# A pre-norm attention and mixture-of-experts layer: four groups of extra PE waits removed

## The reference

```
x = x + attention(layernorm(x))
x = x + ffn(layernorm(x))

attention: 16 heads of 64, q, k, v = split(xh @ Wqkv + bqkv)      # one 64 x 192 matrix for all heads
    att = (q @ k.T / 8) * tril(ones, k=-1)                         # a masked score is 0, not -inf
    out = softmax(att) @ v,  then @ Wr + br
ffn:  w = softmax(flat @ router_w + router_b), all but the top 2 of 8 set to 0
    gelu(flat @ sw1 + sb1) @ sw2 + sb2                             # shared expert, 1024 -> 2048 -> 1024
    + sum over e of w[:, e] * (gelu(flat @ rw1[e] + rb1[e]) @ rw2[e] + rb2[e])
```

## Time and profile before

| | us |
|---|---|
| median of 3 runs | 4011.67 |
| the three runs | 3928.25, 4011.67, 4037.73 |
| time of the profiled execution | 3928.25 |
| its span (slowest core, first to last instruction) | 3926.7 |
| spans of the 8 cores | 3921.7 to 3926.7 |

### The profile page before, as it was taken

The page is one execution under the profiler, slowest core; times in us unless marked ns, Lnnn a source line. Parts: engine busy times, 40 slices in busy tenths (PEclk is TensorE's granted clock), DMA queues, the critical chain, the costliest instruction groups (busy, mean ns, idle before and its releaser), DMA issues.

```text
span 3926.7 us, 45908 instructions; the slowest of 8 cores (3921.7 to 3926.7 us)
## 1 busy us (share of the span) xinstructions
PE 2935.5 (75%) x15380; PEld 1345.2 (34%) x15380; DVE 1167.6 (30%) x2358; ACT 855.8 (22%) x1354; POOL 28.9 (1%) x55
## 2 busy tenths in 40 slices
PE   2454454555455445665999999999999999999997
PEld 0122222222222222222444444444444444444443
DVE  5222222222222222253132333333233333333332
ACT  0232222332222223101212121121212112122210
POOL 0000000000000000000000000000000000000000
PEclk7555555555555555686999999999999999999998
DMA  2100000000000000050022220502222050221302
GB/s 87 33 1 1 1 1 1 1 1 1 1 1 1 1 1 1 1 86 1 1 48 39 44 44 1 87 1 44 43 38 49 1 86 1 44 43 33 54 1 86
DMA packets 7087, 98.81 MB, mean 25 GB/s; under 512 B 1860, under 2 KB 2260, under 8 KB 2260
## 3 DMA queue, kind: packets, MB, share of 16 engines
q0 software_dynamic: 3984, 77.81, 11.8%
q1 hardware_dynamic: 2884, 18.06, 1.3%
HBM read 165.10 MB, written 8.39 MB: 44 GB/s over the span
## 4 chain that ended last, share of the span: by engine, by line
PE 70%; DVE 12%; issue 8%; ACT 7%; DMA 1%; DVEq 1%; ACTq 0%; SPq 0%; POOL 0%
PE PM L746 26%; PE PM L835 25%; PE PS L438 6%; DVE SMASK L418 5%; ACT PT L423 4%; PE PS L399 4%; ACT PT L409 3%; DVE AVN L455 2%; PE PTR L462 2%; PE PS L342 2%; PE PS L505 2%; DVE RZ L450 1%; PE PS L368 1%; PE PS L359 1%; DVE XLN L248 1%
## 5 line engine op out<-in xcount | busy, mean ns | idle before, releaser
L746 PE MATMUL PM<-XLN,W 128*128 128x512 bf16 x4608 | 1020.7, 385 | 0.7 <-DVE WSB L704 0.7
L835 PE MATMUL PM<-H1G,W 128*128 128x512 bf16 x4608 | 999.0, 379 | 0.0
L763 ACT ACTIVATE H1G<-PM,B1C 128x512 bf16<-128x512 f32 x576 | 395.9, 687 | 1611.6 <-PE PM L746 1611.6
L746 PEld LDWEIGHTS PM<-XLN,W 128*128 128x128 bf16 x4608 | 455.3, 99 | 562.6 <-issue 33.6
L835 PEld LDWEIGHTS PM<-H1G,W 128*128 128x128 bf16 x4608 | 450.9, 98 | 543.7
L438 PE MATMUL PS<-VA,PT 128*128 128x65 bf16 x2560 | 176.2, 242 | 349.5 <-ACT PT L423 349.5
L812 DVE TENSOR_TENSOR H1G<-H1G,WB 128x512 bf16<-128x512 bf16 x512 | 217.8, 425 | 686.3 <-ACT H1G L763 686.3
L850 DVE TENSOR_TENSOR XRES<-XRES,PM 128x512 f32<-128x512 f32 x288 | 198.2, 688 | 652.1 <-PE PM L835 652.1
L399 PE MATMUL PS<-QT,KT 64*128 64x512 bf16 x640 | 322.4, 600 | 73.0 <-ACT PT L409 72.4
L409 ACT ACTIVATE PT<-PS 128x512 bf16<-128x512 f32 x384 | 209.0, 594 | 566.6 <-PE PS L399 566.1
L418 DVE TENSOR_TENSOR SMASK<-PS,MASKS 128x512 f32<-128x512 f32 x256 | 176.9, 691 | 457.9 <-PE PS L399 285.1
(11 more groups left out here) (99 smaller groups left out, 826.7 us busy)
## 6 DMA issues: line engine op xcount, KB each, us to landing
W<-w1cat POOLq DMA_DIRECT2D x9, 4096.0 KB, 28.7
W<-w2cat POOLq DMA_DIRECT2D x9, 4096.0 KB, 28.8
XRES<-xt SPq DMA_DIRECT2D x8, 1024.0 KB
ot<-XRES SPq DMA_DIRECT2D x8, 1024.0 KB
WRF<-wr_rl POOLq DMA_DIRECT2D x1, 2048.0 KB, 17.2
MASKS<-c_masks SPq DMA_DIRECT2D x1, 1024.0 KB
B1C<-b1col POOLq DMA_DIRECT2D x9, 8.0 KB, 28.1
B2C<-b2col_t POOLq DMA_DIRECT2D x9, 4.0 KB, 2.6
```

Source lines behind the costliest of these rows:

```text
L746: lambda e, psv=psv, kc=kc, ht=ht, tt=tt: e.matmul(psv, W1[:, kc * DFF + ht * 128: kc * DFF + (ht + 1) * 128], xln(kc)[:, tt * 512:(tt + 1 ...
L763: lambda e, h1sl=h1sl, psv=psv, e_i=e_i, ht=ht: e.activation(h1sl, psv, AF.Gelu, bias=B1C[:, (e_i % 2) * 16 + ht: (e_i % 2) * 16 + ht + 1]),
L835: lambda e, psv=psv, kc=kc, dtl=dtl, buf=buf: e.matmul(psv, W2[:, kc * D + dtl * 128: kc * D + (dtl + 1) * 128], H1G[:, buf * 8192 + kc * 512:
```

## The change

It takes four waits off TensorE's instructions and nothing else. No instruction is added, dropped or put in another place. What is left: a score matmul waits for its slot alone; the first matmul of an mm1 or mm2 tile waits for its slot and its input; a broadcast matmul waits for the DMA of its row and its slot. The same kind of wait in the output projection (L505) stays.

```diff
                             w = [slot_free[slot]]
-                            if len(sc_hist) >= 2:
-                                w.append(sc_hist[-2])
...
                                 w = [pm1_free[slot]]
-                                if len(sg_hist) >= 2:
-                                    w.append(("SS", sg_hist[-2]))
...
                                 w = [pm2_free[slot], h1_ready]
-                                if len(vx_hist) >= 2:
-                                    w.append(("SV", vx_hist[-2]))
...
-                                    waits=[("WRS", gq_wrow), pm1_free[r],
-                                           ("SS", C["SS"]), ("SV", C["SV"])],
+                                    waits=[("WRS", gq_wrow), pm1_free[r]],
```

## The result

| | before | after |
|---|---|---|
| median of 12 runs each, us | 4037.16 | 3858.24 |
| lowest and highest run, us | 3928.25 to 4349.9 | 3804.15 to 4231.92 |
| ratio after to before | | 0.9741, 95% interval 0.966 to 0.9822 |
| the same on the chip of run 10 below (11 and 7 runs) | | 0.9666, 95% interval 0.9645 to 0.9686 |

What follows compares the result with a forecast made beforehand. Attention was taken as bound by a chain of waits with no engine full, experts by a busy TensorE. Savings of 82 + 34 + 9 = 125 us off 3928.25 gave 3804 us, -3.2%, range 3770 to 3890.

Steps and rivals of the forecast that it cites:

- Part 1: Attention's unmasked exps: without the wait they run 0.49 us apart, saving 5.13 us per head, 82 us in all.
- Rival (a): Attention: ScalarE streams exps more slowly, 0.58 to 0.60 us apart, giving 3833 to 3841 us; chance 0.13.
- rival (b): Exps stream at the scores' pace and the clock stays up at seams, giving 3768 to 3775 us; chance 0.08.
- rival (d): Attention: PSUM writes by scores and reads by ScalarE shut each other out, making it slower, 4042 us; chance 0.03.
- Rival (c): Attention: another wait, such as the slot's, holds the scores, so nothing is gained there, 3885 us; chance 0.08.
- Part 2: Tiles inside an expert: the waits on gelu and add had always been met, so removing them is worth nothing.
- Part 3: Seams between experts: broadcasts no longer wait on VectorE, saving 4.2 us a seam, 34 us for eight.
- Part 4: TensorE's clock behind the seams: half the loss from its fall regained, 1.1 us a seam, 9 us for eight.
- the starting level of the sum: Whole kernel: the savings of 125 us were subtracted from the profiled execution's 3928.25 us, giving 3804.
- the other level (3887): Whole kernel: the time expected if the new runs' median sits as high above their profiled execution as before.

Runs made afterwards that it cites:

- run 10: The changed kernel unaltered, measured again beside the kernel before on another chip: ratio 0.9666, median of 7 runs 3807.23 us against 3936.68.
- run 1: The kernel before with only the score matmuls' wait on the last unmasked exp but one removed: ratio 0.9799.
- Run 5: The kernel before with score matmuls waiting for the unmasked exp three back instead of two back: ratio 0.9794, median span 3845.9 us.
- run 3: The kernel before with only the product tiles' waits on the last gelu but one and last add but one removed: ratio 0.9992.
- Run 4: The kernel before with the ScalarE and VectorE waits removed from three of the four seam broadcasts, the first keeping them: ratio 0.9919, median span 3897.7 us.
- run 2: The kernel before with only the four seam broadcasts' waits on ScalarE and VectorE removed: ratio 0.9862, median span 3887.6 us.
- run 7: The changed kernel with the next expert's broadcasts and copies issued ahead of the last output block: ratio 0.9608, median span 3775 us.

## Why the prediction was right or wrong

**Part 1 was right.** 5.13 us a head and 82 in all were forecast; 83.5 came, by the start of the projection, and 83 in run 1. The 0.49 us that two neighbouring exps showed in the trace before is also the pace of twelve in a row, 0.488, and the block's stretch was forecast at 6.08 us and measured at 6.08. That this is ScalarE's pace is shown by the changed kernel: its exps wait for a score once per block, the eight scores on the chain come 0.42 us apart ((3.54 - 0.60) / 7), and the exps stay at 0.49. Run 5 agrees but proves less, since its loop could give 0.47. Rival (a), a slower stream as that of the exps' neighbours with a bias operand, rival (b), exps at the pace of the scores, and rival (d), that writing and reading PSUM shut each other out, are refuted by the 0.488; the exps did get longer (median 597 to 616 ns) but not further apart. Rival (c) is refuted by run 1. The one element per cycle of the Trainium skill, "ScalarE: Activation LUTs", section "Step-by-step: what each stage is for" (the prediction named the heading just before it), is a rate "once the pipe fills", inside one instruction; the 0.43 us and 102 us worked out from it left out whatever each instruction adds. For exps of 128x512 with a score ready for each, 0.488 was measured, and no run shows where the 0.06 go.

**Part 2 was right:** run 3, 0.9992.

**Part 3 was right:** a seam of 2.7 us in place of 6.9, 4.2 gained, 34 in all. (Every second seam of the kernel before was 0.2 us shorter than the one that was read, so 33 is closer.) Run 4 adds that most of it lay in the serial rounds and not in the wait for the bias add.

**Part 4 was mis-sized.** I took half of the mean loss of 2.1 us, 1.1 a seam. In the trace of the changed kernel the clock falls at every seam, on all eight cores, and what became shorter is the stretch: 10 matmuls in 3.8 us behind a seam, as at the cheaper of the two seams before, is a loss of 1.6 us, so 0.5 a seam was gained by that count and not 1.1. The experts' stage gained 39.4 us, less 34 of idle time that leaves about 6 of the 9 forecast, and run 2 left 3. That the clock can stay up at a seam, as I had assumed for some, is shown by run 2, whose seams last 2.9 us: at 5 or 6 of eight on cores 0 to 3 and at one on cores 4 to 6.

**The step that failed is the starting level of the sum.** The 125 us that were taken off held: the cores gave 123, six of them ended within 4 us of the forecast 3804, and -3.2% lies inside both intervals. (3928.25 - 125 is 3803, not 3804; the slip changes nothing.) What failed is "off the profiled execution's 3928.25". That execution was the lowest of the three that were shown, 83 us below their median, and I put its level on record as the kernel's time, with a sentence on the other level (3887) and no weight on it. Set beside the median of 4011.67 that stood in the table, 3804 reads as -5.2%, twice what the change is worth, 2.6% to 3.3%. The runs showed a median of 3858.24, 54 us above the forecast, and a lowest of 3804.15: the sum had forecast the best of 12 executions and not the middle one. That 3858 lies inside the range is owed to the upper end, which was drawn wide for rival (c) and the higher level, and not to the sum. The time of a kernel on eight cores is that of the slowest, and how often all of them are undisturbed differed between the chips: in 2 of 12 executions of the changed kernel here, in 5 of 7 in run 10. The better start was the median: 4011.67 x 0.968 = 3883, with the range going down from there. It would have been 25 us too high, so the level stays uncertain either way; the ratio is what could be forecast well.

Not tried: whether the long stretches at 0.81 come more or less often with the denser attention, and what sets them off. The 12 and 7 executions of the changed kernel and the 12 and 11 of the one before don't settle it.

## What to carry to other kernels

When a chain of waits alternates two engines, count how many items the wait lets into the loop: its length divided by that number is the pace, until an engine's own pace, read from two neighbours that did overlap, takes over. One more in flight was enough here, and the next serial loop of the same shape was worth twice as much as the one removed. A wait that was always met cost nothing measurable here, so look for waits by the idle time ahead of them and not by their number. And say which level of a spread of runs a forecast is for: work the change out on the trace, as a ratio, and apply it to the median of the runs if it is the median that you forecast.

## What was not expected

On the chip of runs 1 to 8 the cores 0 to 3 show a short stretch below full clock some time behind a seam. Run 1, the same stretch of the same code on core 0 and on core 4; columns as above:

```profile
1988.00:1993.00 5.00, 5.00 (x23) 2.10 (x21) 0.98 (x3) 2.04 (x3) 0.00 (x0) 0.88 1.10 190
```

```profile
1988.00:1993.00 5.00, 5.00 (x25) 2.29 (x24) 1.28 (x3) 1.88 (x4) 0.00 (x0) 1.00 0.83 141
```

Core 0 has a clock of 0.88 and 23 matmuls, core 4 has 1.00 and 25. Core 0 has such a stretch, of some 6 us at 0.81, behind all eight seams, 48 us in all, which costs 9 us; cores 4 to 7 have none. It also stays at half clock for longer, 78 us over the eight seams against 65 to 68. Both are part of the 13 us between the dies in run 1, and of the 9 in run 3. In run 7, where the clock never falls between experts, no core has such a stretch and all eight end within 4.5 us of each other.

It is not the return from half clock alone that brings the stretch. In run 2, whose seams last 2.9 us, core 0 shows it behind seven of the eight seams but falls to half clock at only two. One of the other six, from just before the seam:

```profile
2505.20:2508.20 3.00, 2.56 (x12) 0.81 (x10) 1.12 (x2) 0.00 (x0) 0.00 (x0) 1.00 0.00 0
2508.20:2519.20 11.00, 9.48 (x44) 4.38 (x46) 4.50 (x9) 3.34 (x5) 1.07 (x2) 1.00 0.83 136
2519.30:2525.30 6.00, 5.91 (x24) 2.50 (x23) 1.28 (x3) 1.98 (x3) 0.00 (x0) 0.81 0.97 165
```

So a stop between experts can cost three times: the idle time, a stretch at half clock, and on the cores of some dies a stretch at 0.81 some 10 us later. What sets off the third is not shown; the traces of the first result have none behind their seams, before or after.
